# A depthwise 5x5 convolution on TensorE: the images become the stationary operand, the filter matrix the moving one, and the input arrives in transfers of 112 and 9 partitions

## The reference

```python
ch = x.shape[-1]
k = jnp.transpose(kernel, (1, 2, 0))[:, :, None, :]
y = lax.conv_general_dilated(x, k, window_strides=(1, 1), padding='SAME',
                             dimension_numbers=('NHWC', 'HWIO', 'NHWC'), feature_group_count=ch)
return x + y
```

## Time and profile before

| | us |
|---|---|
| median of 3 runs | 959.04 (958.02 to 959.66) |
| span of the profiled execution, first to last instruction | 956.4 |
| TensorE busy in it | 936.2 |
| VectorE busy | 647.5 |
| ScalarE busy | 635.0 |
| GpSimd busy | 1.9 |

### The profile page before, as it was taken

One profiled execution on the slowest core, in us unless ns is written; L12 is line 12 of the kernel. 1 busy time (PEld: TensorE's weight loads), 2 busy tenths in 40 slices (PEclk: granted clock), 3 DMA queues, 4 the chain that ended last, 5 costly groups with the idle time before them and its releaser, 6 DMA issues.

```text
span 956.4 us, 12191 instructions
## 1 busy us (share of the span) xinstructions
PE 936.2 (98%) x4032; PEld 732.0 (77%) x4032; DVE 647.5 (68%) x1034; ACT 635.0 (66%) x482; POOL 1.9 (0%) x9
## 2 busy tenths in 40 slices
PE   4999999999999999999999999999999999999997
PEld 3777777777777777777777777777777777777775
DVE  6676667676676766666767767676666676676761
ACT  4666767676766667676767666676767676666764
POOL 0000000000000000000000000000000000000000
PEclk9999999999999999999999999999999999999999
DMA  9999999999999999999999999999999999999965
GB/s 362 363 361 359 366 353 372 364 364 366 351 373 366 347 371 358 355 361 362 375 364 368 360 345 384 358 352 360 360 368 360 361 375 365 362 370 352 374 223 168
DMA packets 41717, 339.03 MB, mean 354 GB/s; under 512 B 4720, under 2 KB 7792, under 8 KB 29424
## 3 DMA queue, kind: packets, MB, share of 16 engines
q1 hardware_dynamic: 41712, 338.97, 96.8%
HBM read 184.81 MB, written 154.14 MB: 354 GB/s over the span
## 4 chain that ended last, share of the span: by engine, by line
PE 98%; DMA 1%; DVE 1%; ACT 0%; issue 0%; SPq 0%; DVEq 0%
PE sums L332 98%; DMA band_in<-filters 1%; DVE x_low L294 0%; DVE weights L285 0%; ACT y_out L229 0%; SPq L145 0%; DVE band_rest L270 0%; DVE band L273 0%; DVE band L266 0%; DVEq L262 0%
## 5 line engine op out<-in xcount | busy, mean ns | idle before, releaser
L332 PE MATMUL sums<-x_high,weights 128*120 128x512 f32 x2688 | 733.1, 394 | 0.0
L332 PEld LDWEIGHTS sums<-x_high,weights 128*120 128x120 f32 x2688 | 488.3, 182 | 135.3
L229 ACT ACTIVATE y_out<-sums 120x1024 f32<-120x1024 f32 (+1 forms) x288 | 335.9, 1166 | 307.6 <-PE sums L332 307.1
L294 DVE TENSOR_TENSOR x_low<-x_in,x_high 128x2176 fp32r<-128x2176 f32 x192 | 393.3, 2089 | 83.4 <-ACT x_high L219 83.4
L332 PE MATMUL sums<-x_low,weights 128*120 128x512 f32 x1344 | 421.0, 394 | 13.9 <-DVE x_low L294 13.9
L285 DVE CAST weights<-band 32x240 fp32r<-32x240 f32 x768 | 230.7, 381 | 198.5 <-PE sums L332 189.4
L219 ACT ACTIVATE x_high<-x_in 128x2176 fp32r<-128x2176 f32 x192 | 336.4, 1752 | 8.3 <-DMA x_in<-x 8.3
L332 PEld LDWEIGHTS sums<-x_low,weights 128*120 128x120 f32 x1344 | 243.7, 181 | 82.3 <-issue 13.9
L266 DVE TENSOR_TENSOR band<-band_in,residual 128x180 fp32r<-128x180 f32 x24 | 8.2, 340 | 6.2 <-DMA band_in<-filters 6.2
L270 DVE TENSOR_TENSOR band_rest<-band,residual 128x180 f32<-128x180 f32 x24 | 8.3, 346 | 0.8
L273 DVE TENSOR_TENSOR band<-band_in,band_rest 128x180 fp32r<-128x180 f32 x24 | 8.3, 346 | 0.8
## 6 DMA issues: line engine op xcount, KB each, us to landing
x_in<-x SPq DMA_DIRECT2D x95, 1856.0 KB, 13.1
y<-y_out SPq DMA_DIRECT2D x192, 784.0 KB, 8.8
band_in<-filters SPq DMA_DIRECT2D x24, 96.0 KB
x_in<-x SPq DMA_DIRECT2D x1, 1088.0 KB, 5.8
x_in<-x SPq DMA_DIRECT2D x1, 768.0 KB, 7.6
```

The costliest lines, as they stand in the source:

```text
L229: act.activation(y_out[k % Y_SLOTS][:, a * CHUNK:b * CHUNK], psum[0:OUT_PARTS, a:b, :].rearrange("p b n -> p (b n)"), ACT.Copy).then_inc(b ...
L294: dve.tensor_tensor(x_low[slot][:, a:b], x_in[k][:, a:b], x_high[slot][:, a:b].bitcast(F32), ALU.subtract).then_inc(low_ready[slot], 1)
L332: product = pe.matmul(psum[0:OUT_PARTS, bank, :], weights[slot][:, w, side * OUT_PARTS:(side + 1) * OUT_PARTS], v[slot][:, first:first + C ...
```

## The change

The kernel is written anew round another tiling. The reference, the splitting in high and low, and the three products stay.

**Operands.** The image is cut into 5 x 5 squares of 11 x 11 pixels. A partition holds one of the 121 pixels of a square; the free axis holds 25 squares x 128 images. A square's 121 x 128 block of x is now the stationary operand (128 columns, the images), and the filter matrix is the moving operand: for each of the 121 pixels, the outputs of the square and of a rim of two pixels round it. So a product writes 128 images (partitions) x 13 or 15 rows x 14 or 16 columns of output. A channel takes 25 squares x 3 products = 75 matmuls of 182, 208, 210 or 240 columns.

**Tiles and seams.** Two or three neighbouring squares of a strip share a bank (13 tiles a channel, 8 banks in rotation), and their sums add up in PSUM. Where tiles overlap, ScalarE copies the part that no tile wrote before (`copy_strip`), and VectorE adds the overlap to what is in `y_out` (`add_seams`, 19 additions a channel).

**The filter matrix.** GpSimd makes it: every 4 channels it splits the taps (`split_taps`), and for each channel it multiplies them with masks (`make_matrix`: two operations of 100 elements a partition, two of 300).

**Splitting x.** VectorE makes the first fifth of `x_high` (`cast_high`) and all of `x_low`, in three pieces; ScalarE makes the rest of `x_high` in two pieces.

**Transfers.** A channel's input is 121 partitions x 12,800 B without padding rows, issued as a transfer of 112 partitions and one of 9 (`PARTS`). Its output is one transfer of 128 partitions x 12,160 B. `x_in` has four buffers, `y_out` three.

Core of the diff (the whole file is replaced; of the old code one part stands for all):

```diff
-parts = [(w, v) for w, v in ((HIGH, x_low), (LOW, x_high), (HIGH, x_high))]
-product = pe.matmul(psum[0:OUT_PARTS, bank, :],
-                    weights[slot][:, w, side * OUT_PARTS:(side + 1) * OUT_PARTS],
-                    v[slot][:, first:first + CHUNK],
-                    start=n == 0, stop=n == len(products) - 1)
+SQUARE = 11
+BANKS, BANK = 8, 512
+PIECES = ((0, 1), (1, 3), (3, 5))
+X_SLOTS = 4
+SLOTS = 2
+Y_SLOTS = 3
+PARTS = ((0, 112), (112, PIXELS))
...
+            def load_x(c):
+                if c >= X_SLOTS:
+                    sp.wait_ge(low_ready, len(PIECES) * (c - X_SLOTS + 1))
+                for a, b in PARTS:
+                    sp.dma_start(x_in[c % X_SLOTS][a:b, :], x[c, a:b, :]).then_inc(x_loaded[c % X_SLOTS], 16)
+            def store_y(c):
+                sp.wait_ge(added, ADDS * (c + 1))
+                sp.dma_start(out[c, :, :], y_out[c % Y_SLOTS][:, :]).then_inc(y_stored[c % Y_SLOTS], 16)
+            for c in range(CHANNELS):
+                if c + X_SLOTS < CHANNELS:
+                    load_x(c + X_SLOTS)
+                if c:
+                    store_y(c - 1)
...
+            def make_matrix(c):
+                for part in (HIGH, LOW):
+                    pool.tensor_tensor(expanded, taps, across, ALU.mult)        # 100 elements
...
+                if c >= SLOTS:
+                    pool.wait_ge(sums_done, TILE_COUNT * (c - SLOTS + 1))
+                for part in (HIGH, LOW):
+                    pool.tensor_tensor(matrix, expanded, down, ALU.mult)        # 300 elements
...
+            def copy_strip(c, strip):
+                for t in strip_tiles(strip):
+                    act.wait_ge(sums_done, TILE_COUNT * c + t + 1)
+                    if t == 0 and c >= Y_SLOTS:
+                        act.wait_ge(y_stored[c % Y_SLOTS], 16 * (c // Y_SLOTS))
+                    act.activation(outputs(c, rows, cols), sums(c, t, rows, cols), ACT.Copy).then_inc(copied, 1)
...
+            def add_seams(c, strip):
+                for t in strip_tiles(strip):
+                    dve.wait_ge(copied, TILE_COUNT * c + t + 1)
+                    if ADDS * c + ADDS_BEFORE[t]:
+                        dve.wait_ge(added, ADDS * c + ADDS_BEFORE[t])
+                            dve.tensor_tensor(y, sums(c, t, rows, cols), y, ALU.add).then_inc(added, 1)
+            for c in range(CHANNELS):
+                following = c + 1 < CHANNELS
+                add_seams(c, 0)
+                if following:
+                    cast_high(c + 1)
+                    split_low(c + 1, 0)
+                add_seams(c, 1)
+                if following:
+                    split_low(c + 1, 1)
+                add_seams(c, 2)
+                if following:
+                    split_low(c + 1, 2)
+                add_seams(c, 3)
+                add_seams(c, 4)
...
+            for c in range(CHANNELS):
+                pe.wait_ge(matrix_step, 4 * (c + 1))
+                for t, tile in enumerate(TILES):
+                    wait_bank(c, t)
+                    for k in tile["squares"]:
+                        pe.matmul(target, x_low[c % SLOTS][0:PIXELS, at:at + IMAGES],
+                                  window(c, strip, k, slice(HIGH, HIGH + 1)).squeeze(1), ...)
+                        for part in (LOW, HIGH):
+                            product = pe.matmul(target, x_high[c % SLOTS][0:PIXELS, at:at + IMAGES],
+                                                window(c, strip, k, slice(part, part + 1)).squeeze(1), ...)
+                    product.then_inc(sums_done, 1)
```

More of the change, by code:

```diff
@@ L37 @@
 P = 128
[L39 to L56, removed]
@@ L77 @@
[L77 to L84, removed]
-SLOTS = 2
[L86 to L100, removed]
+SQUARE = 11
+ACROSS = SIDE // SQUARE
+PIXELS = SQUARE * SQUARE
@@ L103, in build, with adds_of @@
+TILES = tiles_of_plane()
+TILE_COUNT = len(TILES)
+def adds_of(tile):
+    return (tile["seam_rows"] > tile["top"]) + (tile["seam_cols"] > tile["lo"])
+ADDS_BEFORE = [sum(adds_of(t) for t in TILES[:n]) for n in range(TILE_COUNT + 1)]
+ADDS = ADDS_BEFORE[-1]
+LAST_STORES = ((0, 3), (3, 4), (4, 5))
+def build(nc, consts, later, x, out):
     with ExitStack() as ctx:
@@ L120, in build @@
-        residual = sbuf("residual", [P, TAP_COLS], F32)
+        y_out = [sbuf(f"y_out{i}", [P, OUT_COLS], F32) for i in range(Y_SLOTS)]
+        matrix = [sbuf(f"matrix{i}", [P, 2, MATRIX], F32R) for i in range(SLOTS)]
+        first = sbuf("first", [P, CONSTS], F32)
+        rest = sbuf("rest", [P, LATER], F32)
+        taps = sbuf("taps", [P, 2, GROUP * FILTER], F32R)
+        spare = sbuf("spare", [P, GROUP * FILTER], F32)
+        expanded = sbuf("expanded", [P, 2, EXPANDED], F32)
         warm = sbuf("warm", [P, 1], F32)
@@ L131, in build @@
[L131 to L153, removed]
+        at = GROUP * FILTER
@@ new lines, in build @@
+        centre = first[0:PIXELS, at:at + FILTER]
+        across = first[0:PIXELS, at + FILTER:at + FILTER + ROW]
+        down = first[0:PIXELS, at + FILTER + ROW:CONSTS]
+        consts_loaded, later_loaded, warm_zeroed, warmed, pads_zeroed = (
+            sem(n) for n in ("consts_loaded", "later_loaded", "warm_zeroed", "warmed", "pads_zeroed"))
+        first_loaded = [sem(f"first_loaded{i}") for i in range(len(PIECES) - 1)]
+        x_loaded = [sem(f"x_loaded{i}") for i in range(X_SLOTS)]
@@ new lines, in build, with piece_cols, bank_of @@
+        y_stored = [sem(f"y_stored{i}") for i in range(Y_SLOTS)]
+        taps_step, matrix_step = sem("taps_step"), sem("matrix_step")
+        cast_done, high_ready, low_ready = sem("cast_done"), sem("high_ready"), sem("low_ready")
+        sums_done, copied, added = sem("sums_done"), sem("copied"), sem("added")
+        def piece_cols(piece):
+            a, b = PIECES[piece]
+            return slice(a * STRIP_COLS, b * STRIP_COLS)
+        def bank_of(c, t):
+            return (c * TILE_COUNT + t) % BANKS
@@ L155, in build, with strip_tiles @@
+        def strip_tiles(strip):
+            return [t for t in range(TILE_COUNT) if TILES[t]["strip"] == strip]
         block = ctx.enter_context(nc.Block())
@@ L158, in _ @@
         def _(sp):
[L159 to L171, removed]
@@ L174, in _ @@
[L174 to L184, removed]
@@ new lines, in _ @@
+            load_x(1)
+            sp.dma_start(rest[:, :], later[:, :]).then_inc(later_loaded, 16)
+            for c in range(2, X_SLOTS):
+                load_x(c)
+            for c in range(CHANNELS):
[3 more added lines that the diff above has]
+                    store_y(c - 1)
+            c = CHANNELS - 1
+            for a, b in LAST_STORES:
+                sp.wait_ge(added, ADDS * c + ADDS_BEFORE[strip_tiles(b - 1)[-1] + 1])
+                done = SIDE * start_of(a)
+                end = SIDE * start_of(b) if b < ACROSS else OUT_COLS
+                sp.dma_start(out[c, :, done:end], y_out[c % Y_SLOTS][:, done:end]).then_inc(y_stored[c % Y_SLOTS], 16)
@@ L221, in empty_banks @@
[L221 to L227, removed]
-                a, b = GROUPS[g]
-                act.activation(y_out[k % Y_SLOTS][:, a * CHUNK:b * CHUNK],
-                               psum[0:OUT_PARTS, a:b, :].rearrange("p b n -> p (b n)"),
-                               ACT.Copy).then_inc(banks_empty[g], 1)
```

363 lines of the change are left out of this document (202 added, 161 removed).

## The result

The changed kernel takes 904.92 us in the median of its runs (903.76 to 904.97 in three), against 958.90 before: a ratio of 0.943, interval 0.942 to 0.945. It is 5.7% faster; 870 was forecast, so a little over half of the 9% forecast came.

The account below looks back on a forecast made before the run. TensorE and the transfers were taken to bound the kernel before, VectorE the new one: 96 channels at 8.9 us (854.4) plus 15.4 for start, end and time outside the span gave 870 us; range 832 to 975.

Parts of the forecast that it names:

- the likeliest case: VectorE sets the pace near 8.9 us a channel, 840 to 920 us in all; chance 0.40.
- TensorE and the transfers are both full: Kernel before: TensorE busy 936.2 of 956.4 us, DMA share 0.99 at 362 GB/s; whatever relieves one must relieve the other.
- The rival that transfers set the pace: Transfers, not VectorE, are slowest: 8.34 to 8.74 us a channel, 816 to 854 us; chance 0.20.
- The rule on unequal engines: Input loads of 112 and 9 partitions: nine DMA engines carry 16 rows, seven 15; the fullest would give 8.74 us.
- the seven: VectorE additions that follow another of their tile without a wait, each saving 0.09 us, 0.6 us a channel.
- the rival of GpSimd: VectorE kept out by GpSimd, or dear PSUM reads: 8.9 plus 0.7 to 1.8 us, 937 to 1043; chance 0.13.
- The fixed part: TensorE: each matmul adds 0.019 us to its columns at 2.4 GHz, 8.15 us a channel for 75 matmuls.
- my two bounds of 0.09 and 0.154 for the load: TensorE's stationary operand load in us: 0.09 if scaled to the higher clock level, 0.154 if not scaled.
- The slower cases beyond 0.131 on average: TensorE's matmul cost does not shrink with width: 11.6 or 17.4 us a channel, 1124 or 1686 us; chance 0.12.

Follow-up runs that it names:

- with 112 and 16: The changed kernel with its input padded to 128 partitions, loaded in two transfers of 112 and 16 partitions: 902.5 and 915.6 us, ratio 0.960 to the kernel before.
- the padded kernel: The changed kernel with its input padded by seven rows of zeros to 128 partitions and loaded in one transfer: 846.13 us, ratio 0.882 to the kernel before.
- the stretches alone: TensorE only, no convolution: stretches of 240 matmuls with a new stationary operand each; 15x16 took 0.1133 us a matmul, 13x14 0.1116.
- the one without the 9 partitions: The changed kernel with the 9-partition transfer left out from the fifth channel on, so the output is another: 857.2 and 857.7 us.

## Why the prediction was right and where it was not

The number came inside the likeliest case, 840 to 920, partly by luck. That case said that VectorE alone would set the pace, at 8.9 us. In 47 channels VectorE did, at 8.94, but as 8.55 of its own and 0.4 lost to GpSimd, which the sum had left out; and in 30 others transfers held the kernel up.

**Transfers.** The step that failed: 3.105 MB "at 362.5 GB/s" is 8.57 us. The bytes were right and the rate wrong; it fell to 337 (9.21 us), and the loads alone to 240 instead of 440. I took a rate from transfers of 128 partitions in and 112 out for transfers of 112 and 9 in and 128 out. Nor is 362.5 shown to be what those transfers can do: it is 3.53 MB in the 9.75 us that TensorE took, and "TensorE and the transfers are both full" read a share of 0.99 as a limit, while ScalarE waited for an input three times only. Even the earlier trace rows held the hint, 440 GB/s for loads of 128 and 323 for stores of 112, which I read as the two directions' rates; alone, stores of 128 run at 426. The rival that transfers set the pace was right in kind, and its price (816 to 854) wrong by this factor. The rule on unequal engines was not the reason: with 112 and 16 the loss stayed. Its 8.74 us is also a wrong sum; 16 rows on the fullest engine against 15.56 on average, on 8.57, are 8.81.

**VectorE.** Predicted 8.9 us a channel; measured 8.55 to 8.6 where nothing disturbs it, and 8.94 where GpSimd does. The additions at 0.23 us on average were sized right (228 ns), the piece of 640 too (0.84); the cast was 0.5 instead of 0.6. A wait on its own last result costs 0.104 us instead of 0.04, but more starts than the seven overlap with the operation ahead, by 0.08 us each. PSUM reads were not dear. So the rival of GpSimd was true as a mechanism, at a quarter of its upper price.

**TensorE.** Predicted 0.109 us a matmul, measured 0.116 in the padded kernel (833.5 us busy for 7200): 8.65 us a channel instead of 8.15. The fixed part was 0.013 instead of 0.019, but narrow matmuls stood at 0.112, between my two bounds of 0.09 and 0.154 for the load. From the stretches alone (27 matmuls at 0.1133, 48 at 0.1116) a channel would be 8.42. Of the 0.23 us more, 0.13 lies in the third square of the three middle strips, where the two matmuls with `x_high` stand 0.135 us apart in the padded kernel's trace; why is open. The slower cases beyond 0.131 on average are excluded.

**ScalarE and GpSimd.** 6.2 us a channel (596 / 96), just under the forecast's 6.4 to 8.0. GpSimd 0.70 us for 300 elements undisturbed and 0.46 for 100, against 0.6 and 0.2; hidden, as forecast, but for the 0.4 us above.

**Start and end.** First matmul at 7.03 us (forecast 6.5). What the sum had no term for is the time after it: the first five channels take 62.6 us, 18 more than at 8.94, because the loads that fill the buffers run at 247 GB/s, one store is waited for 9.0 us, and the clock falls after these waits. The padded kernel loses 3 us there.

**The sum.** Against 854.4 for 96 channels at 8.9, they took 891.4. The first five took 18.1 more than 5 x 8.9, the 25 later ones of 9.1 us and over 17.8 more, and all the others together 1.1 more, since 8.94 is so near the forecast. Start, end and the time outside the span together are 1.8 less than forecast. So 870 became 905 in 30 channels that transfers held up. All of it goes with the shape of the loads, 112 partitions and a small transfer behind them, which the padded kernel removes.

## What to carry to other kernels

Load and store all 128 partitions in one transfer, and pad for it if need be: 7 rows of zeros made this kernel 59 us faster than their absence. Of these, 47 came back by leaving out the small second transfer alone. A full share of the DMA engines doesn't make a rate a limit: three kernels here stood at one with about 346, 362 and 369 GB/s, in each the bytes of a channel over TensorE's time for it. Look for who waits for a transfer, and take the limit from transfers of the same shape alone. When several engines are within 8% of each other (8.55, 8.65 and 9.2 us here), relieving one that isn't last gives nothing, and relieving the last gives only the distance to the next.

## What was not expected of the hardware

A load of 112 partitions is slower than one of 128 in time, not only in rate: 60 against 47 us for twelve. A transfer of 9 partitions behind it adds 1.4 us to 5.0. Matmuls of 182 and of 240 columns with a new stationary operand of 128 columns each take nearly the same, 0.112 and 0.113 us. And two engines that shut each other out can lock in step for many channels: 8.94 us a channel in one kernel, 8.64 in another with the same instructions on both engines. Why they fall in step in one and not in the other is not settled; every trace that did had transfers holding up its first channels, but so had the one without the 9 partitions, which ran at 8.64 nearly throughout.
